# State-space stage with side products in halves over a chunk's four parts and a unit product of 384 columns; stage set-up of semaphores by five engines

## The chip, the cores and the metric

The kernel runs on one core of a Trainium2 chip. A core has TensorE (PE), VectorE (DVE), ScalarE (ACT), GpSimd (POOL) and SyncE (SP), each with a queue of its own that runs in order; they wait for each other through semaphores. The metric is the device time of one execution in microseconds (us); lower is better. 0.2% of it is 13 us.

## What is computed

The reference is two transformer-like layers over x of 128 rows of 64 tokens with 128 features. The change bears on the first block, a state-space block:

```python
normed = rmsnorm(x, input_norm_w)
xp = normed @ in_proj_W
x_z, z = (xp[..., :E], xp[..., E:])                       # E = 256
xc = silu(conv(x_z, conv_W) + conv_b)                     # four taps along time
dt = clip(softplus(xc @ dt_W + dt_b), 0.001, 0.1)
Bp, Cp = xc @ B_W, xc @ C_W                               # 64 states
A = -exp(A_log)
def step(h, x_t, dt_t, B_t, C_t):                         # 64 steps in time, one after the other
    h = exp(dt_t[..., None] * A) * h + dt_t[..., None] * B_t[:, None, :] * x_t[..., None]
    return h, einsum('ben,bn->be', h, C_t)
x = x + (y * silu(z)) @ out_proj_W
```

After it come a gated MLP, attention over a context, attention and a mixture of eight experts, grouped-query attention, attention with a mask, and a mixture of encoder layers.

## The kernel before

The program is a row of 14 stages. Each stage allocates its semaphores (`Stage.semaphore`, line 78), passes a barrier of all engines (`begin`, line 66), runs, clears the semaphores and passes a second barrier. A freshly allocated semaphore is raised to 1 by an instruction of GpSimd, one for each, between the two barriers.

The state-space stage (`mamba`, line 900) takes 16 chunks of 512 tokens (8 rows of 64 tokens). A chunk has 64 steps in time, which the code cuts in four parts j of 16 steps tl. For one step the state of 8 rows, 256 channels and 64 states lies as 128 partitions x 1024 columns in two PSUM banks; two pairs of banks take turns. A unit is the work of one step:

- PE: `products` multiplies the step sizes out to 1024 columns (line 1149, into the banks DT) and the input dt x B (line 1164, into the state's banks); `add_decayed` (by_quarters, line 1132) adds the decayed state of the columns `PE_PART`, with an identity as weights; `contract` (line 1181) multiplies the state products by C into the bank YB.
- ACT: `decay` (line 1381), the exponential of the step sizes into dA, three units ahead.
- DVE: `decay_pe_part` (line 1739) multiplies dA and the state for `PE_PART`; `decay_part` (line 1746) does so for the two `DVE_PARTS`; `add_part` (line 1755) adds the decayed state for these two in PSUM.

`PE_PART` is 256 columns and `DVE_PARTS` are 512 and 256 (lines 1020 and 1021). DVE's order in a unit t is: product of `PE_PART` (t), the two additions (t-1), the two products (t). It waits before the first of these for PE's `add_decayed` of unit t-1. PE's input product of unit t+1 waits for DVE's last product of unit t.

Between the units PE does side products for what comes next, all in the one bank PJ, so that ACT must copy each result out before the next is written: `turn` (transposes x), `conv` (four taps, one of 512 columns at a time), `gates` (z, 256 columns), `project_dt`, `project_c`, `turn_u` and `project_bc` (the parts' inputs), `turn_y` and `project_out` (the output). Their places are written out by hand in `chunk` for each engine: in part 0 dt (tl 7 to 10) and C (12, 13) of the next chunk; in part 2 the turn (8) and the first half of the channels' conv (10 to 13) of the chunk after that; in part 3 the second half (7 to 10) and the gates (11 to 15). ACT's copies stand at steps of their own, after `decay` of the same step. Where a product is copied out one unit and the bank used in the next, PE waits: this is called a hand-over below.

GpSimd multiplies the gates (`gated`), and makes the step size (`step_size`, line 1600) from the dt product in 11 instructions over 1024 columns, of which three add a constant to `lp` (line 1621). It splits the inputs in three bf16 pieces. SP loads x and the residual and spreads the pieces over partitions by 21 DMAs a part (`spread_pieces`).

`loop` runs chunk 0, then a hardware loop of three rounds with four chunks each, then the last three chunks.

Of the kernel before, what the change touches and what calls it, by code (L numbers as in the profile page):

```python
# [58 lines left out]
class Stage:  # L59


    def __init__(self, nc, sems, mem, name):
        self.nc, self.mem, self.name, self.handles = nc, mem, name, []
        mem.callback(self.end)
# [835 lines left out]
def mamba(nc, sems, ps, dram, x_in, x_out):  # L900
# [5 lines left out]
    LP_STEPS = 11  # L906
# [3 lines left out]
    with ExitStack() as mem:  # L910
# [67 lines left out]
        in_done = st.counter("in_done", 4)  # L978
        in_taken = st.counter("in_taken", 4)
        tanh_ready = st.counter("tanh_ready", 4)  # L980
        xz_scaled = st.counter("xz_scaled", 4)
        xz_ready = st.counter("xz_ready", 4)
# [5 lines left out]
        lp_step = st.counter("lp_step", LP_STEPS)  # L988
# [31 lines left out]
        PE_PART = slice(768, 1024)  # L1020
        DVE_PARTS = [slice(0, 512), slice(512, 768)]
# [16 lines left out]
        def loop(eng, chunk, first, last):  # L1038
            first()
            chunk(0, 0, True, True, False)  # L1040
            with looped(nc, eng, 0, (CHUNKS - 4) // 4) as r:
                for v in range(4):
                    chunk(4 * r + (1 + v), (1 + v) % 2, True, True, True)
            for i in range(CHUNKS - 3, CHUNKS):
                chunk(i, i % 2, i + 1 < CHUNKS, i + 2 < CHUNKS, True)
# [3 lines left out]
        with nc.Block() as block:  # L1049

            @block.sync
            def _(sp):
# [49 lines left out]
                def chunk(i, u, lead, lead2, trail):  # L1102
                    load_res(i, 0)
                    if trail:
                        spread_pieces(i, 1)
                        store(i - 1, 3)
                    load_res(i, 1)
# [6 lines left out]
                    if lead2 and not (isinstance(i, int) and i == CHUNKS - 3):  # L1114
                        load_x(i + 3)
# [12 lines left out]
            def _(pe):  # L1128
# [63 lines left out]
                def conv(i, f, k):  # L1192
                    if k == 0:
                        if f == 0:
                            pe.wait_ge(xT_ready.sem, xT_ready.at(i))
                        else:
                            pe.wait_ge(in_taken.sem, in_taken.at(i, 1))
                    mm = by_quarters(ps[:, PJ, :], w_conv[:, k, 128 * f:128 * f + 128], xT[:, :, k:k + 64], k == 0, k == 3)
                    if k == 3:
                        mm.then_inc(in_done.sem, 1)  # L1200

                def gates(i, j):
                    if j % 2 == 0:
                        pe.wait_ge(in_taken.sem, in_taken.at(i, 2 + j // 2))
# [3 lines left out]
                    if n == 1:  # L1208
                        mm.then_inc(in_done.sem, 1)

                def project_dt(i, u, e, f):
                    if e == 0:
                        pe.wait_ge(xz_ready.sem, xz_ready.at(i, f + 1))
                    if f == 0:
                        if e == 1:
                            pe.wait_ge(dtp_taken.sem, dtp_taken.at(i, 1))
                    mm = by_quarters(ps[:, PJ, :], w_dt[:, f, 128 * e:128 * e + 128], xz[:, u, 512 * f:512 * f + 512],
                                     f == 0, f == 1)
                    if f == 1:
                        mm.then_inc(dtp_done.sem, 1)  # L1220

                def project_c(i, u, f):
                    if f == 0:
                        pe.wait_ge(dtp_taken.sem, dtp_taken.at(i))
                    mm = by_quarters(ps[:, PJ, :], w_c2[:, f], xz[:, u, 512 * f:512 * f + 512], f == 0, f == 1)
                    if f == 1:
# [28 lines left out]
                def first():  # L1255
# [4 lines left out]
                    for i in range(2):  # L1260
# [3 lines left out]
                        for f in range(2):  # L1264
                            for k in range(4):
# [2760 lines left out]
```

## Time and profile before

| what | us |
|---|---|
| median of 3 runs | 6489.89 (6489.69 to 6494.92) |
| the profiled execution | 6484.01 |
| span of its trace | 6482.2 |
| end of the state-space stage | 2404 |

The profile is of one execution. Its page gives the busy share of each engine, the span in 40 slices and the costliest groups of instructions. The trace behind it answers as a timeline (start, length, instruction, and in brackets the idle time before it with what ended it), as groups by line, and as a table of windows. A PE row of "x8" holds 4 weight loads and 4 matmuls or 8 matmuls that were merged; the lengths of matmuls are modelled and overlap, so the distance from one start to the next is what counts. DVE rows overlap by some 0.06 us, for the same reason.

### The profile page before, as it was taken

The page shows a single profiled execution, that of the slowest core. Times are in us where ns is not written, and L with a number is a line of the kernel's source. Part 1 is how long each engine was busy: PE and PEld are TensorE (multiplying, and loading weights), DVE is VectorE, ACT ScalarE, POOL GpSimd, SP SyncE. Part 2 cuts the span into 40 slices and gives each one's busy share as a digit, 9 for nine tenths or more (in the row PEclk, how much of TensorE's full clock was granted, in tenths as well). Part 3 has the DMA queues.
Part 4 walks back from the last instruction along what each step waited for, and adds up shares of the span by engine and source line. Part 5 has one row for each costly group of instructions (what it writes and reads, how often), then busy time and mean ns, then how long its engine had stood idle before and what let it go on. Part 6 is the DMA issues. An engine that isn't in the chain of part 4 may idle for free. (4 is left out here: it accounts for less than half of the span.)

```text
span 6482.2 us, 173452 instructions
## 1 busy us (share of the span) xinstructions
PE 5026.5 (78%) x60580; PEld 2983.8 (46%) x60580; DVE 4987.2 (77%) x10255; ACT 3330.0 (51%) x4888; POOL 3321.4 (51%) x3031
## 2 busy tenths in 40 slices
PE   4889888988889875886868966999856648777890
PEld 1333333333333333564655534666645436666440
DVE  2999999999999984897965355777679928888334
ACT  3666666666666643555741202444446517777440
POOL 6544444545444413665634573555523329888443
PEclk8999999999999997998979977999978859999995
DMA  1111111111111112221123631000011012222443
GB/s 39 46 48 46 50 42 50 42 50 43 50 47 44 48 47 78 56 57 34 42 67 101 142 107 34 17 17 17 12 36 31 26 52 73 72 75 71 128 131 104
DMA packets 620485, 368.02 MB, mean 57 GB/s; under 512 B 67337, under 2 KB 601292, under 8 KB 619852
## 3 DMA queue, kind: packets, MB, share of 16 engines
q1 hardware_dynamic: 600524, 335.54, 18.6%
q0 software_dynamic: 11648, 21.26, 1.7%
q8 instruction: 352, 5.77, 0.4%
q10 hardware_dynamic: 7680, 3.15, 0.2%
q14 instruction: 281, 2.30, 0.1%
HBM read 204.83 MB, written 66.85 MB: 42 GB/s over the span
## 5 line engine op out<-in xcount | busy, mean ns | idle before, releaser
L1381 ACT ACTIVATE mb_dA<-ps,mb_a_neg 128x1024 f32<-128x1024 f32 x1008 | 1123.1, 1114 | 852.1 <-PE ps L1149 693.7
L1746 DVE TENSOR_TENSOR mb_m<-mb_dA,ps 128x512 f32<-128x512 f32 x2016 | 1015.6, 543 | 0.0
L1755 DVE TENSOR_TENSOR ps<-mb_m,ps 128x512 f32<-128x512 f32 x1984 | 1008.8, 552 | 0.0
L1132 PE MATMUL ps<-mb_m,mb_ident 128*32 128x256 f32 x7936 | 637.3, 393 | 2.9 <-DVE mb_m L1739 1.7
L1181 PE MATMUL ps<-mb_m,mb_cz 128*32 128x256 f32 x8064 | 624.3, 381 | 17.2 <-DVE mb_m L1746 6.5
L1164 PE MATMUL ps<-mb_ur,mb_bl 64*128 64x256 bf16 x4032 | 391.6, 273 | 160.3 <-DVE mb_m L1746 155.3
L1739 DVE TENSOR_TENSOR mb_m<-mb_dA,ps 128x256 f32<-128x256 f32 x1008 | 413.9, 411 | 72.0 <-PE ps L1132 45.0
L1149 PE MATMUL ps<-mb_ur,mb_sel 64*128 64x256 bf16 x4032 | 397.7, 276 | 28.6 <-DMA mb_ur<-mb_pc 15.6
L1181 PEld LDWEIGHTS ps<-mb_m,mb_cz 128*32 128x32 f32 x8064 | 256.1, 110 | 206.9 <-issue 34.7
L677 POOL TENSOR_TENSOR x_p<-x_p,x_rec 128x2048 f32<-128x2048 f32 x64 | 231.7, 3620 | 211.4 <-DVE x_rec L838 211.4
L1149 PEld LDWEIGHTS ps<-mb_ur,mb_sel 64*128 64x128 bf16 x4032 | 115.1, 94 | 485.0 <-ACT mb_dA L1381 288.1
L1164 PEld LDWEIGHTS ps<-mb_ur,mb_bl 64*128 64x128 bf16 x4032 | 156.8, 94 | 311.1 <-DVE mb_m L1746 298.3
L1660 POOL TENSOR_TENSOR mb_ys<-mb_ys,mb_cbu 128x256 f32<-128x256 f32 x64 | 46.8, 732 | 472.9 <-ACT mb_ys L1471 472.9
L677 POOL TENSOR_TENSOR ea_p<-ea_p,ea_rec 128x2048 f32<-128x2048 f32 x70 | 253.5, 3621 | 39.7 <-DVE ea_rec L838 39.1
L3187 POOL TENSOR_TENSOR gq_qr<-gq_qc,gq_qs 128x1024 f32<-128x1024 f32 x64 | 150.9, 2358 | 237.1 <-DVE gq_qs L3234 219.8
L1132 PEld LDWEIGHTS ps<-mb_m,mb_ident 128*32 128x32 f32 x7936 | 156.5, 108 | 217.9 <-DVE mb_m L1739 124.6
L2518 POOL DMA_INDIRECT mx_tk<-moe_normed,moe_tokens x156 | 147.5, 945 | 163.1 <-POOLq L68 103.3
L487 PE MATMUL ps<-x_ident,x_p 128*128 128x128 f32 x1024 | 164.1, 312 | 64.3 <-POOL x_p L677 64.3
L599 ACT ACTIVATE x_p<-x_p 128x2048 f32<-128x2048 f32 x64 | 122.0, 1906 | 166.3 <-DVE x_p L828 166.3
L606 ACT COPY x_pT<-ps 128x1024 f32<-128x1024 f32 x128 | 129.2, 1009 | 138.1 <-PE ps L487 137.1
L1647 POOL TENSOR_TENSOR mb_rest<-mb_tm,mb_pc 128x768 f32<-128x768 f32 x64 | 105.6, 1650 | 184.4 <-ACT mb_pc L1449 184.4
L606 ACT COPY ea_pT<-ps 128x1024 f32<-128x1024 f32 x140 | 141.6, 1012 | 99.4 <-PE ps L487 97.5
(493 smaller groups left out, 13198.9 us busy)
## 6 DMA issues: line engine op xcount, KB each, us to landing
mb_ur<-mb_pc SPq DMA_DIRECT2D x768, 64.0 KB
mb_bl<-mb_pc SPq DMA_DIRECT2D x576, 64.0 KB
ef_w<-in_ef_w SPq DMA_DIRECT2D x35, 514.5 KB
mx_w<-in_mx_w SPq DMA_DIRECT2D x39, 384.0 KB
moe_made<-mx_y SPq DMA_DIRECT2D x39, 256.0 KB, 2.4
ea_wqk<-in_ea_wqk SPq DMA_DIRECT2D x70, 129.0 KB
ea_wvo<-in_ea_wvo SPq DMA_DIRECT2D x70, 128.5 KB, 2.1
ea_x<-hidden SPq DMA_DIRECT2D x280, 32.0 KB, 2.0
```

The lines of the kernel that those rows point to most:

```text
L487: mm = nc.tensor.transpose(ps[:, 6 + c0 // 512, c0 % 512:c0 % 512 + 128], P_g[:, u, g, t, 2 * jj:2 * jj + 2, :].rearrange("p h k -> p (h k ...
L606: nc.scalar.copy(pT[:, t], ps[:, 6:8, :].rearrange("p a n -> p (a n)")).then_inc(pT_ready.sem, 1)
L677: nc.gpsimd.tensor_tensor(v, v, rec[:].rearrange("p (c a) -> p c a", a=1).to_broadcast([128, 32, 64]), ALU.mult).then_inc(p_ready.sem, 1)
L1132: mm = nc.tensor.matmul(out[c:c + 32], weights[:, c:c + 32], moving, start=start, stop=stop, skip_group_check=not grouped)
L1149: mm = nc.tensor.matmul(ps[:, DT + g, 256 * pl:256 * pl + 256], sel[k, pl], ur[k, t // 16 % 2, t % 16], start=True, stop=True)
L1164: mm = nc.tensor.matmul(ps[:, UB + 2 * ((t + v) % 2) + g, 256 * pl:256 * pl + 256], bl[k, s, tl, 128 * pl:128 * pl + 128], ur[k, s, tl], s ...
L1181: mm = nc.tensor.matmul(ps[32 * pr:32 * pr + 32, YB, 0:E], cz[:, j % 2, pr, 32 * tl:32 * tl + 32], m[:, t % RING, 256 * pr:256 * pr + 256] ...
L1381: nc.scalar.activation(dA[:, t % RING].rearrange("p (g n) -> p g n", g=2), ps[:, DT:DT + 2, :], ACT.Exp, scale=a_neg[:, 0:1]).then_inc(dA_ ...
L1739: nc.vector.tensor_tensor(m[:, t % RING, PE_PART], dA[:, t % RING, PE_PART], state(u, t - 1, PE_PART), ALU.mult).then_inc(mp_ready.sem, 1)
L1746: nc.vector.tensor_tensor(m[:, t % RING, cols], dA[:, t % RING, cols], state(u, t - 1, cols), ALU.mult).then_inc(md_ready.sem, 1)
L1755: nc.vector.tensor_tensor(h, m[:, t % RING, cols], h, ALU.add).then_inc(hd_ready.sem, 1)
L3187: nc.gpsimd.tensor_tensor(qr[:, t], qc[:, t], qs[:, t], ALU.add).then_inc(q_turned.sem, 1)
```

## The change

1. `PE_PART` becomes 384 columns, `DVE_PARTS` 320 and 320.
2. conv, dt and C products are made in halves of 256 columns, one a step, at steps 8 to 15. The parts change: part 0 has the turn, the gates and the first three quarters of C; part 1 the last of C and the conv of the first channels; part 2 the conv of the others; part 3 dt. x and z have semaphores of their own. dt, conv and gates are made two chunks ahead, C one; the dt products of chunk 1 are made before chunk 0 starts.
3. ACT's copies and tanh, and GpSimd's gates and norm, move with them. GpSimd makes the step size in two halves of 512 columns, 22 instructions, and adds the constants as `p * 1.0 + c`.
4. SP loads x of chunk i+3 earlier in chunk i.
5. A new semaphore is raised by GpSimd, SP, ACT, DVE and PE in turn.
6. Three later stages (experts, join, grouped-query attention) load their weights from ACT's queue in place of SP's.

```diff
     def semaphore(self, name):
         sem = self.nc.alloc_semaphore(name=f"{self.name}_{name}")
+        self.engines[len(self.handles) % 5].sem_inc(sem, 1)
         self.handles.append(sem)
-        self.nc.gpsimd.sem_inc(sem, 1)
...
-        PE_PART = slice(768, 1024)
-        DVE_PARTS = [slice(0, 512), slice(512, 768)]
+        PE_PART = slice(640, 1024)
+        DVE_PARTS = [slice(0, 320), slice(320, 640)]
...
-                def conv(i, f, k):
...
-                    mm = by_quarters(ps[:, PJ, :], w_conv[:, k, 128 * f:128 * f + 128], xT[:, :, k:k + 64], k == 0, k == 3)
+                def conv_tap(i, f, n):
+                    half, k = n // 4, n % 4
...
+                    mm = by_quarters(ps[:, PJ, cols], w_conv[:, k, 128 * f:128 * f + 128], xT[:, rows, k:k + 64],
+                                     k == 0, k == 3)
...
+                def side(i, u, j, tl, lead, trail):
...
+                        if j == 0 and lead:
+                            pe.wait_ge(dtp_taken.sem, dtp_taken.at(i + 1))
+                        elif j == 1 and lead:
+                            pe.wait_ge(cn_ready.sem, cn_ready.at(i + 1))
+                        elif j >= 2 and lead >= 2:
+                            pe.wait_ge(conv_taken.sem, conv_taken.at(i + 2, j - 1))
...
+                    if j == 0:
+                        if lead >= 2:
+                            if tl == 8:
+                                turn(i + 2)
...
+                            if tl in (10, 11, 12, 13):
+                                gates(i + 2, tl - 10)
+                        if lead and tl == 14:
+                            if lead >= 2:
+                                pe.wait_ge(gates_taken.sem, gates_taken.at(i + 2))
+                            project_c(i + 1, 1 - u, 0)
+                            project_c(i + 1, 1 - u, 1)
+                        if lead and tl == 15:
+                            project_c(i + 1, 1 - u, 2)
+                    elif j == 1:
+                        if lead and tl == 0:
+                            project_c(i + 1, 1 - u, 3)
+                        if lead >= 2 and tl >= 8:
+                            conv_tap(i + 2, 0, tl - 8)
+                    elif lead >= 2 and tl >= 8:
+                        if j == 2:
+                            conv_tap(i + 2, 1, tl - 8)
+                        else:
+                            project_dt(i + 2, u, (tl - 8) // 4, (tl - 8) % 4)
...
+                                ins = nc.gpsimd.tensor_scalar(p, p, 1.0, LOG1P[4 - n // 2], ALU.mult, ALU.add)
```

A unit with a side product on PE, in a chunk before (part 3, step 7, where the second channels' conv begins):

```order
L1132 MATMUL ps<-mb_m,mb_ident 32x256 [waits mb_mp_ready]
L1132 MATMUL ps<-mb_m,mb_ident 32x256 x3
L1181 MATMUL ps<-mb_m,mb_cz 32x256 [waits mb_md_ready,mb_mp_ready]
L1181 MATMUL ps<-mb_m,mb_cz 32x256 x3
L1132 MATMUL ps<-mb_xT,mb_w_conv 32x512 [waits mb_in_taken,mb_y_ready]
L1132 MATMUL ps<-mb_xT,mb_w_conv 32x512 x3
L1149 MATMUL ps<-mb_ur,mb_sel 128x256 [waits mb_dA_ready]
L1149 MATMUL ps<-mb_ur,mb_sel 128x256 x3
L1164 MATMUL ps<-mb_ur,mb_bl 128x256 [waits mb_md_ready]
L1164 MATMUL ps<-mb_ur,mb_bl 128x256 x3
```

The same engine now, in part 3, step 12, where the second column of dt begins:

```order
L1139 MATMUL ps<-mb_m,mb_ident 32x384 [waits mb_mp_ready]
L1139 MATMUL ps<-mb_m,mb_ident 32x384 x3
L1188 MATMUL ps<-mb_m,mb_cz 32x256 [waits mb_md_ready,mb_mp_ready]
L1188 MATMUL ps<-mb_m,mb_cz 32x256 x3
L1139 MATMUL ps<-mb_xz,mb_w_dt 32x256 [waits mb_dtp_taken]
L1139 MATMUL ps<-mb_xz,mb_w_dt 32x256 x3
L1156 MATMUL ps<-mb_ur,mb_sel 128x256 [waits mb_dA_ready]
L1156 MATMUL ps<-mb_ur,mb_sel 128x256 x3
L1171 MATMUL ps<-mb_ur,mb_bl 128x256 [waits mb_md_ready]
L1171 MATMUL ps<-mb_ur,mb_bl 128x256 x3
```

The added decay has 384 columns, the side product 256, and it waits for ACT's copy of the unit before; ahead of it nothing of PE's can run. On DVE, two units before:

```order
L1739 TENSOR_TENSOR mb_m<-mb_dA,ps 128x256 [waits mb_hp_ready,mb_y_summed,mb_dA_ready]
L1755 TENSOR_TENSOR ps<-mb_m,ps 128x512 [waits mb_md_ready,mb_ub_done]
L1755 TENSOR_TENSOR ps<-mb_m,ps 128x256 [waits mb_md_ready]
L1746 TENSOR_TENSOR mb_m<-mb_dA,ps 128x512 [waits mb_hd_ready]
L1746 TENSOR_TENSOR mb_m<-mb_dA,ps 128x256 [waits mb_hd_ready]
```

and now:

```order
L1784 TENSOR_TENSOR mb_m<-mb_dA,ps 128x384 [waits mb_hp_ready,mb_y_summed,mb_dA_ready]
L1800 TENSOR_TENSOR ps<-mb_m,ps 128x320 [waits mb_md_ready,mb_ub_done]
L1800 TENSOR_TENSOR ps<-mb_m,ps 128x320 [waits mb_md_ready]
L1791 TENSOR_TENSOR mb_m<-mb_dA,ps 128x320 [waits mb_hd_ready] x2
```

The order is the same and so are the waits; only the widths moved. On ACT, at the end of part 0 now, the copies of the gates and of C stand one behind the other in the units (L1397 is the exponential of a unit):

```order
L1397 ACTIVATE mb_dA<-ps,mb_a_neg 128x1024 [waits mb_md_ready,mb_dt_done] x2
L1427 ACTIVATE mb_raw<-ps 128x512 [waits mb_z_ready,mb_gates_done]
L1397 ACTIVATE mb_dA<-ps,mb_a_neg 128x1024 [waits mb_md_ready,mb_dt_done] x2
L1427 ACTIVATE mb_raw<-ps 128x512 [waits mb_z_ready,mb_gates_done]
L1397 ACTIVATE mb_dA<-ps,mb_a_neg 128x1024 [waits mb_md_ready,mb_dt_done] x3
L1445 COPY mb_cn<-ps 128x512 [waits mb_cz_ready,mb_c_proj]
L1494 COPY mb_ys<-ps 128x256 [waits mb_yzT_done,mb_y_summed]
```

Before, dt and C stood in this part and the gates in part 3; each copy still comes behind the exponential of its unit.

## Rows read from the trace of the kernel before

**Rows 1.** The page, section 1: busy us, share of the span and instructions by engine.

```profile
PE 5026.5 (78%) x60580; PEld 2983.8 (46%) x60580; DVE 4987.2 (77%) x10255; ACT 3330.0 (51%) x4888; POOL 3321.4 (51%) x3031
```

**Rows 2.** Table of windows: window and length in us, busy (instructions) by engine, PEclk, DMA.

```profile
484.00:626.00 142.00, 127.35 (x1816) 53.79 (x1813) 139.33 (x323) 90.96 (x117) 67.84 (x53) 1.00 0.18 47
```

**Rows 3.** Line L1583, once a chunk: ns min/median/max, and start of first and last.

```profile
L1583 POOL TENSOR_TENSOR mb_nrstd<-mb_nrstd,mb_half_neg x1: 1041/1041/1041, 1616.8 to 1616.8; 128x4 f32<-128x4 f32 x1
...
L1583 POOL TENSOR_TENSOR mb_nrstd<-mb_nrstd,mb_half_neg x1: 1041/1041/1041, 1758.3 to 1758.3; 128x4 f32<-128x4 f32 x1
```

**Rows 4.** Timeline of DVE, one unit: start us, length us, instructions, idle before.

```profile
938.00 0.41 DVE L1739 TENSOR_TENSOR mb_m<-mb_dA,ps 128x256 f32<-128x256 f32 x1
...
940.19 0.41 DVE L1739 TENSOR_TENSOR mb_m<-mb_dA,ps 128x256 f32<-128x256 f32 x1
```

**Rows 5.** Timeline of PE: a unit with a whole side product, hand-overs, a half one.

```profile
949.15 0.65 PE L1132 MATMUL ps<-mb_w_bc,mb_xz 128*32 128x128 f32 x16 [0.54 <-ACT mb_tm L1435]
949.72 0.39 PE L1149 MATMUL ps<-mb_ur,mb_sel 64*128 64x256 bf16 x4
...
965.10 0.39 PE L1149 MATMUL ps<-mb_ur,mb_sel 64*128 64x256 bf16 x4
965.33 0.38 PE L1164 MATMUL ps<-mb_ur,mb_bl 64*128 64x256 bf16 x4
965.64 0.64 PE L1132 MATMUL ps<-mb_m,mb_ident 128*32 128x256 f32 x8
966.10 0.61 PE L1181 MATMUL ps<-mb_m,mb_cz 128*32 128x256 f32 x8
966.53 1.04 PE L1132 MATMUL ps<-mb_xT,mb_w_conv 128*32 128x512 f32 x8
967.51 0.39 PE L1149 MATMUL ps<-mb_ur,mb_sel 64*128 64x256 bf16 x4
...
969.76 0.64 PE L1132 MATMUL ps<-mb_w_in,mb_xT_tok 128*32 128x256 f32 x8 [0.65 <-ACT mb_raw L1403]
...
971.76 0.62 PE L1132 MATMUL ps<-mb_w_in,mb_xT_tok 128*32 128x256 f32 x8
972.31 0.39 PE L1149 MATMUL ps<-mb_ur,mb_sel 64*128 64x256 bf16 x4
```

**Rows 6.** Timeline of DVE: its waits at the change of chunk and later.

```profile
980.22 0.42 DVE L1739 TENSOR_TENSOR mb_m<-mb_dA,ps 128x256 f32<-128x256 f32 x1 [0.72 <-PE ps L1132]
...
1002.00 0.42 DVE L1739 TENSOR_TENSOR mb_m<-mb_dA,ps 128x256 f32<-128x256 f32 x1 [0.46 <-PE ps L1132]
```

**Rows 7.** Groups of DVE, 300 to 2200 us: count, busy us, mean ns, idle before.

```profile
L1755 DVE TENSOR_TENSOR ps<-mb_m,ps 128x512 f32<-128x512 f32 x829 | 568.3, 686 | 0.0
L1755 DVE TENSOR_TENSOR ps<-mb_m,ps 128x256 f32<-128x256 f32 x829 | 347.5, 419 | 0.0
```

**Rows 8.** Where the loop enters anew: a window, then DVE's timeline.

```profile
836.00:840.00 4.00, 3.15 (x24) 1.36 (x20) 2.28 (x5) 1.95 (x4) 1.45 (x2) 0.50 0.34 89
...
837.35 0.42 DVE L1739 TENSOR_TENSOR mb_m<-mb_dA,ps 128x256 f32<-128x256 f32 x1 [2.83 <-PE ps L1132]
```

**Rows 9.** Timeline of GpSimd and PE in the stage's start.

```profile
65.07 1.05 POOL L1617 TENSOR_SCALAR mb_lp<-mb_ex 128x1024 f32<-128x1024 f32 x1 [0.20 <-POOL mb_ex L1615]
...
68.76 2.78 POOL L1621 TENSOR_SCALAR mb_lp<-mb_lp 128x1024 f32<-128x1024 f32 x1 [0.20 <-POOL mb_lp L1609]
...
91.18 1.09 PE L1233 MATMUL ps<-mb_ident,mb_du 128*128 128x128 f32 x4 [15.26 <-POOL mb_du L1611]
```

**Rows 10.** Line L81, the increments: the first stage, then all stages.

```profile
L81 POOLq EVENT_SEMAPHORE  x56: 17/17/17, 0.9 to 5.2; - x56
...
L81 POOLq EVENT_SEMAPHORE  x524: 17/17/17, 0.9 to 6317.0; - x175
```

**Rows 11.** Timeline of the grouped-query stage's start.

```profile
3910.79 0.35 SPq L2913 DMA_DIRECT2D gq_ident<-in_ident  x1
...
3914.51 0.43 SPq L2917 DMA_DIRECT2D gq_x<-hidden  x1
```

More of the change, by code:

```diff
@@ L1100, in first, with chunk @@
                     spread_pieces(0, 1)
-                def chunk(i, u, lead, lead2, trail):
+                def chunk(i, u, lead, trail):
                     load_res(i, 0)
@@ L1286, in chunk @@
+                def chunk(i, u, lead, trail):
                     for t in range(T):
-                        j, tl = t // 16, t % 16
-                        k = 4 * i + j
                         if 1 <= t < T - 1:
@@ L1348, in chunk @@
[L1348 to L1360 removed]
+                        side(i, u, t // 16, t % 16, lead, trail)
@@ L1494, in first @@
                             take_conv(i, f)
+                            tanh_of_x(i, i, f)
+                        if i == 0:
+                            for e in range(2):
+                                take_dt(0, e)
                         for half in range(2):
@@ L1510, in first, with chunk @@
                     decay(0, 2)
-                def chunk(i, u, lead, lead2, trail):
+                    for e in range(2):
+                        take_dt(1, e)
+                    for j in range(4):
+                        norm(2, j)
+                def chunk(i, u, lead, trail):
                     for t in range(T):
@@ L1684, in first, with chunk @@
                         split_lo(0, j)
-                def chunk(i, u, lead, lead2, trail):
+                    for f in range(2):
+                        gate_x(1, 1, f)
+                    norm_scale(2)
+                    step_size(1, 1, 0, 4)
+                def chunk(i, u, lead, trail):
                     for t in range(T):
                         j, tl = t // 16, t % 16
+                        if j == 0 and tl == 2 and lead >= 2:
+                            scale(i + 2)
                         if tl == 1 and (j > 0 or trail):
@@ L1772, in first, with chunk @@
                     weigh_bc(0, 1)
-                def chunk(i, u, lead, lead2, trail):
-                    for t in range(T):
+                def chunk(i, u, lead, trail):
+                    for t in range(1, T):
                         j, tl = t // 16, t % 16
-                        if t >= 1:
-                            decay_pe_part(i, u, t)
+                        decay_pe_part(i, u, t)
                         if t >= 2:
@@ L2565, in _ @@
             def _(act):
+                for dst, src in loads:
+                    act.dma_start(dst, src).then_inc(w_loaded.sem, 16)
                 def take(i):
@@ L2727, in _ @@
             def _(act):
+                for dst, src in loads:
+                    act.dma_start(dst, src).then_inc(w_loaded.sem, 16)
                 for i in range(CHUNKS):
@@ L2911, in _ @@
             def _(sp):
-                for dst, src in loads:
-                    sp.dma_start(dst, src).then_inc(w_loaded.sem, 16)
                 def lead(i, u):
@@ L3102, in _ @@
             def _(act):
+                for dst, src in loads:
+                    act.dma_start(dst, src).then_inc(w_loaded.sem, 16)
                 def take_x(i, u):
```

396 lines of the change are left out of this document (194 added, 202 removed).

## Prediction

> **What bounds the kernel now.** I read the page first [rows 1]: in the span of 6482.2 us PE is 78% and DVE 77% busy, no engine at its limit over the whole. So the question is the state-space stage, the first 2400 us, and there the table of windows [rows 2]: in 142 us DVE works 139.33 us, PE shows 127.35 and the granted clock is 1.00. DVE is the bound of this stage. One chunk (512 tokens, 63 units) takes 141.5 us: the once-a-chunk power of the norm stands at 1616.8 and at 1758.3 [rows 3]. The DVE timeline [rows 4] shows a unit without waits, from one first product to the next: 938.00 to 940.19, 2.19 us. PE's own unit, from rows where it never waits for DVE [rows 5], is step size 0.23 (965.10 to 965.33), input 0.31, added decay 0.46, contraction 0.43: 1.43 us. A side product of 512 columns adds 0.98 (966.53 to 967.51), so a unit with one takes 2.41, more than DVE's 2.19; one of 256 columns adds 0.55 (971.76 to 972.31). PE has slack in the sum (1.43 x 63 plus the side work, against 141.5) but not in such stretches, and DVE's few waits are for PE [rows 6]: 0.72 at the change of chunk, 0.46 in the stretch of dt products.
>
> **Unit product of 384 columns.** Of DVE's five instructions a unit the three products together stay at 1024 columns; the two additions fall from 768 to 640. 512 against 256 columns is 686 against 419 ns [rows 7]: 267 ns for 256 columns, so 128 columns are 133 ns. With 62 additions a chunk DVE falls by 8.2 us, from 139.3 to 131.1. On PE the added decay grows by 128 columns. A side product shows the price of 256 columns, 0.98 less 0.55 = 0.43 [rows 5], so 128 are 0.21 us: the unit goes to 1.64.
>
> The Trainium skill (VectorE: DVE Perf Modes, The TRN2 errata) speaks against this edit: it tells us to keep tiles at 512 columns or more, since each instruction pays a fixed part. Here the count of instructions stays at five, and rows of this trace give the fixed part either way, so the sum is 8.2 by the row and 8.3 by the page's slope of one column in 1/0.96 ns; I take the row.
>
> **Side products in halves.** Per chunk PE then has: 63 x (0.23+0.31+0.43) = 61.1; 62 x 0.67 = 41.5; 32 half products (16 conv, 8 dt, 4 gates, 4 C) x 0.55 = 17.6; 17 short steps (turns, B/C, output) at the price of the B/C projection, 0.57 (949.15 to 949.72) [rows 5], 9.7. Sum 129.9, one per cent under DVE's 131.1: the two engines tie. What is not hidden then are PE's waits for ACT. A bank handed over (PE product, ACT copy, PE again) shows 0.65 idle at 969.76, and the B/C projection 0.54 at 949.15 [rows 5]. The new order has a hand-over from one unit to the next in four places a chunk (between the two dt columns, between the halves of the gates, gates to C, C to the turn) and four B/C projections. PE reaches them 0.2 later than now, which leaves about 0.6 and 0.5 each: 4 x 0.6 + 4 x 0.5 = 4.4. On the other side PE can't run ahead of DVE, since the input product waits for DVE's last product of the unit: in units 3, 5 and 7 of each part, which have no side work (1.64 against 2.06), it gains 0.42 each, 1.26 a part, and can use of this only the lag of some 0.55 that the stretch before has left: 0.7 is lost, 2.9 a chunk. PE's chunk: 129.9 + 4.4 + 2.9 = 137.2; I take 137.5. In DVE's terms these are 6.4 us of waits a chunk where there are 2.2 now. Gain 4.0 a chunk, in 14 chunks 56 us. Bounds: 133.5 (DVE's 131.1 and its present 2.2, the hand-overs hidden) and 141.5 (nothing gained).
> The last two chunks carry next to no side products; there I take DVE's 8.2 less 2: 12 us.
> Three times the loop enters anew; a wait of 2.83 and 4 us at a granted clock of 0.50 are seen there [rows 8], the slow one of the two levels, after PE had stood still. With PE in the lead each of the units at that clock costs more: +4 in all.
> GpSimd gets no slower: its 11 steps become 22 of half width, but the three additions of a constant, 2.77 us, take the form of the multiply-add, 1.05 [rows 9]. SyncE's four x loads come earlier in its queue, ahead of the second spread of pieces, which waits for unit 12 of PE anyway: nothing. ACT's count of copies is unchanged.
>
> **Start of the stage.** PE's first turn of u stands 15.26 us for GpSimd's step sizes and starts at 91.18 [rows 9]. The additions' new form saves 3 x 1.7 = 5.2 on that chain, the z gates (5.1) leave it, half-width overheads cost about 2; then eight dt products of the second chunk are put ahead of unit 1, some 5 us at the low clock. Net -4, between -12 and +4.
>
> **Set-up by five engines.** GpSimd issues 524 increments in 14 stage set-ups [rows 10]; the 56 of the first stand from 0.9 to 5.2, 78 ns each, and all other engines stand at the barrier. 524 x 0.08 = 42 us. With a fifth each, in parallel at the same pace, 8.5 us stay: -33. No row shows the pace of another engine's increment. From above the whole 42 can't be beaten by more than its four fifths; from below I take PE at 200 ns, twice and a half GpSimd's, and its 105 then leave 21: -20. I take -33, GpSimd's row being the same instruction.
> The Trainium skill (Advanced Engine Details and Errata, DMA Bandwidth Details) puts an increment's overhead at about one cycle on this chip. By that the set-ups cost nothing now and the change gains nothing there; the forecast would be 33 higher, 6418. The row of 78 ns decides against it, and the page speaks of DMA.
>
> **Weights on ACT's queue.** In the grouped-query stage eight weight loads stand ahead of the first x load: 3910.79 to 3914.51 [rows 11], and PE's first work needs that x load. On two queues that is about -3.5; in the experts' stage two loads are 0.9, mostly hidden; in the join PE starts on the weights themselves: 0. Sum -4, between 0 and -6.
>
> **Sum.** -56 -12 +4 -4 -33 -4 = -105 us. The profiled execution took 6484.01, 1.8 more than its span; it goes to 6379. The median is 5.9 above it: 6489.9 - 105 = 6385.
>
> **Rivals.**
> Hand-overs hidden: PE is late less often than I count, the chunk falls to 133.5, DVE stays the bound. For it: only a wait that ends after DVE's own unit counts, and PE may lag by about 0.6 us before DVE waits. Against it: eight half products in a row use up that lag. 14 x 4 more: 6329.
> PE as the bound without gain: the chunk stays at 141.5 because each PE unit costs 0.07 more than its rows (a switch between two kinds of product). Only set-up, tail and start are won: 6441.
> The other side, slower: the added decay is a link in a chain, DVE product to PE to the next DVE product, and has 0.21 us more in each unit. Its margin is DVE's unit less the input product, the added decay's full length and some 0.2 of signals: 2.19 - 0.31 - 0.64 - 0.2 = 1.0 us now, 2.06 - 0.31 - 0.85 - 0.3 = 0.6 after (0.3, since PE must also wait for a longer DVE product). With each ACT copy that comes late all beyond it goes to DVE. That decides once a chunk takes over 146 us, since the other terms bring 49: all four hand-overs, the B/C projections and 0.1 more in each of the 63 units. At 148 it gives 6489.9 - 49 + 91 = 6532. Against it: no stretch now loses more than 0.8 at a time.
> That set-up isn't won (the increments overlap with the barrier anyhow): 6418.
>
> **Chances.** Forecast 0.50; hand-overs hidden 0.22; no gain in the chunk 0.16; set-up not won 0.06; slower 0.06. The range runs from 6320 to 6448: it takes in 6329 and 6441, and the lower bound of the set-up on the forecast; about 0.06 is left out below and 0.12 above. About 0.2%, 13 us, is what a measurement of this kernel can tell from no change: faster by more 0.92, within it 0.04, slower 0.04.
>
> **What will show it.** Right: the once-a-chunk power every 137 to 138 us; DVE 131 busy of it, its waits at the 384-column product, most of them in units 12 to 18 of the first part and at the change of chunk; PE's idle before the dt, gates, C and turn steps near 0.6; the increments of the first stage done by about 1.8 us; later stages unchanged in length. Wrong: DVE waits under 3 us a chunk (first rival), or the PE unit without side work above 1.70 and with a half above 2.25 (second and third), or barriers that still stand over 2 us.

## The result, and the profile after

The changed kernel takes 6448.17 us (median of 4 runs, 6440.6 to 6455.99) against 6490.6 of the kernel before, measured beside it: a ratio of 0.9933, with a 95% interval from 0.9916 to 0.9951. It is 42 us faster, where the prediction had 105. The range ended at 6448, so the median lies 0.2 above its end, which is within the noise; the gain of 42 in place of 105 is not. The number of the rival "PE as the bound without gain" (6441) is near the measured one, but its mechanism is only a part of what happened: the experiments below show that PE's own work does not fill the chunk.

The chunk first. The once-a-chunk power of the norm (its line is L1606 now; columns as in [rows 3]) stands at:

```profile
L1606 POOL TENSOR_TENSOR mb_nrstd<-mb_nrstd,mb_half_neg x1: 1041/1041/1041, 677.6 to 677.6; 128x4 f32<-128x4 f32 x1
...
L1606 POOL TENSOR_TENSOR mb_nrstd<-mb_nrstd,mb_half_neg x1: 1041/1041/1041, 818.5 to 818.5; 128x4 f32<-128x4 f32 x1
```

That is 140.9 us a chunk, where [rows 3] has 141.5 and the forecast 137.5. The page's first section, as [rows 1]:

```profile
PE 5171.6 (80%) x62372; PEld 3072.5 (48%) x62372; DVE 4875.8 (76%) x10255; ACT 3332.8 (52%) x4888; POOL 3274.3 (51%) x3207
```

and the table of windows over one chunk, as [rows 2]:

```profile
681.00:822.00 141.00, 135.24 (x1918) 59.12 (x1920) 131.94 (x321) 90.59 (x116) 64.89 (x64) 1.00 0.19 47
```

The 139.33 of [rows 2] belong to a window of 142 us. A window of one chunk of the kernel before, 141.5 us, is:

```profile
1187.50:1329.00 141.50, 126.84 (x1804) 53.51 (x1804) 138.83 (x323) 90.46 (x116) 67.83 (x54) 1.00 0.17 47
```

So DVE's work fell from 138.8 to 131.9, by 6.9 us (the forecast had 8.2, from 139.3 to 131.1). But it now stands idle for 9 us of every chunk, where it did for 2.7. The table of waits over the same chunk says for whom (engine, line and product, who released it: us in all, times, longest):

```profile
DVE mb_m L1784 <- PE ps L1139: 8.5, 11, 1.6
PE ps L1188 <- issue: 2.3, 3, 1.1
PE ps L1139 <- ACT mb_tm L1458: 1.3, 4, 0.3
PE ps L1139 <- ACT mb_raw L1427: 0.7, 2, 0.3
PE ps L1156 <- ACT mb_dA L1397: 0.5, 1, 0.5
PE ps L1139 <- ACT mb_ex L1450: 0.4, 1, 0.4
```

DVE waits 8.5 us for PE, and PE in turn waits for ACT's copies. DVE's waits lie at the change of chunk (1.60 and 0.44), at the gates and at C in part 0 (0.20 and 1.02), in the first two units of part 1 (1.49 and 0.58), in those of parts 2 and 3 (0.70 and 0.58 in each), and behind dt (0.56). Two of them:

```profile
683.94 0.56 DVE L1784 TENSOR_TENSOR mb_m<-mb_dA,ps 128x384 f32<-128x384 f32 x1 [1.60 <-PE ps L1139]
...
715.12 0.56 DVE L1784 TENSOR_TENSOR mb_m<-mb_dA,ps 128x384 f32<-128x384 f32 x1 [1.02 <-PE ps L1139]
```
 The largest of PE's waits, at L1188 (the contraction), is put down to "issue", so no name leads to it. PE's timeline at the start of part 1 shows it (columns as in [rows 5]):

```profile
698.29 0.61 PE L1188 MATMUL ps<-mb_m,mb_cz 128*32 128x256 f32 x8
698.83 0.65 PE L1196 MATMUL ps<-mb_ident,mb_xn 128*128 128x128 f32 x4
...
702.40 0.61 PE L1188 MATMUL ps<-mb_m,mb_cz 128*32 128x256 f32 x8
702.83 0.61 PE L1139 MATMUL ps<-mb_w_in,mb_xT_tok 128*32 128x256 f32 x8
...
718.58 0.85 PE L1139 MATMUL ps<-mb_m,mb_ident 128*32 128x384 f32 x8
720.51 0.64 PE L1188 MATMUL ps<-mb_m,mb_cz 128*32 128x256 f32 x8 [1.08 <-issue]
...
728.83 0.85 PE L1139 MATMUL ps<-mb_m,mb_ident 128*32 128x384 f32 x8
729.50 0.61 PE L1188 MATMUL ps<-mb_m,mb_cz 128*32 128x256 f32 x8
730.04 0.39 PE L1156 MATMUL ps<-mb_ur,mb_sel 64*128 64x256 bf16 x4
730.27 0.38 PE L1171 MATMUL ps<-mb_ur,mb_bl 64*128 64x256 bf16 x4
730.58 0.85 PE L1139 MATMUL ps<-mb_m,mb_ident 128*32 128x384 f32 x8
```

and ACT's, just ahead of it:

```profile
718.55 1.11 ACT L1397 ACTIVATE mb_dA<-ps,mb_a_neg 128x1024 f32<-128x1024 f32 x1 [1.08 <-PE ps L1156]
719.57 0.58 ACT L1445 COPY mb_cn<-ps 128x512 f32<-128x512 f32 x1
720.03 0.38 ACT L1494 COPY mb_ys<-ps 128x256 f32<-128x256 f32 x1
```

The first contraction of a part writes the bank YB anew, so it must wait until ACT has copied the last part's sums out (`take_y`, L1494). That copy stands behind an exponential of 1.11, and in part 1 behind the copy of C too. The last rows show a unit of PE without side work: 728.83 to 730.58, 1.75 to 1.77, where the forecast had 1.64. The contraction takes 0.54 there (729.50 to 730.04), and 0.43 ahead of a side product with weights of 128 x 32 like its own (702.40 to 702.83). It takes 0.54 ahead of a transpose too, whose operands are fp32 as its own are but whose weights are 128 x 128 (698.29 to 698.83).

Between the two profiled executions the 43.2 us split so (DVE's first product of a chunk is the mark in the first three rows; the first chunk is in the first row):

| stretch | before | after | difference | forecast |
|---|---|---|---|---|
| start, to the first product of chunk 1 | 264.5 | 259.7 | -4.8 | -4, and -3 of set-up |
| the next 13 chunks | 1850.7 | 1839.0 | -11.7 | -56 (14 chunks) + 4 |
| the last two | 277.9 | 266.6 | -11.3 | -12 |
| from there to the stage's end | 11.3 | 11.1 | -0.2 | 0 |
| the 13 later stages | 4077.9 | 4062.6 | -15.3 | -30 of set-up, -4 of weights |

The first row hides two larger differences. DVE's first product of chunk 0 stands at 118.3 before and at 107.9 after, 10.4 earlier, 2.5 of it from the set-up. Chunk 0 itself, with eight dt products more on PE, takes 151.7 in place of 146.2.

The last row is not a sharp one: the grouped-query stage alone took between 798.6 and 817.8 us in the profiles of changed kernels that don't touch it, so the terms in it are read from medians below.

### The profile page after: what moved, and what is told of

The parts are those of the page before. It is cut to its first block and busy times, and to the rows that moved or that the text cites. A ratio compares the mean times of both kernels' runs of the same rounds, so it can differ in the third digit from the quotient of the medians.

```text
span 6439.0 us, 177583 instructions
## 1 busy us (share of the span) xinstructions
PE 5171.6 (80%) x62372; PEld 3072.5 (48%) x62372; DVE 4875.8 (76%) x10255; ACT 3332.8 (52%) x4888; POOL 3274.3 (51%) x3207
## 5 line engine op out<-in xcount | busy, mean ns | idle before, releaser
L1397 ACT ACTIVATE mb_dA<-ps,mb_a_neg 128x1024 f32<-128x1024 f32 x1008 | 1122.8, 1114 | 826.2 <-PE ps L1156 743.7
L1791 DVE TENSOR_TENSOR mb_m<-mb_dA,ps 128x320 f32<-128x320 f32 x2016 | 886.8, 482 | 0.0
L1800 DVE TENSOR_TENSOR ps<-mb_m,ps 128x320 f32<-128x320 f32 x1984 | 881.3, 491 | 0.0
L1139 PE MATMUL ps<-mb_m,mb_ident 128*32 128x384 f32 x7936 | 847.1, 499 | 12.2 <-DVE mb_m L1784 2.8
L1784 DVE TENSOR_TENSOR mb_m<-mb_dA,ps 128x384 f32<-128x384 f32 x1008 | 555.4, 551 | 166.3 <-PE ps L1139 115.5
L1188 PE MATMUL ps<-mb_m,mb_cz 128*32 128x256 f32 x8064 | 622.1, 380 | 42.4 <-issue 28.4
L1188 PEld LDWEIGHTS ps<-mb_m,mb_cz 128*32 128x32 f32 x8064 | 255.2, 110 | 439.5 <-issue 420.4
L1171 PEld LDWEIGHTS ps<-mb_ur,mb_bl 64*128 64x128 bf16 x4032 | 184.1, 94 | 67.3 <-DVE mb_m L1791 40.5
L3241 POOL TENSOR_TENSOR gq_p<-gq_p,gq_rec 128x2048 f32<-128x2048 f32 x32 | 115.8, 3620 | 128.9 <-DVE gq_rec L3318 128.9
```

The costliest lines, as they stand in the source:

```text
L1139: mm = nc.tensor.matmul(out[c:c + 32], weights[:, c:c + 32], moving, start=start, stop=stop, skip_group_check=not grouped)
L1171: mm = nc.tensor.matmul(ps[:, UB + 2 * ((t + v) % 2) + g, 256 * pl:256 * pl + 256], bl[k, s, tl, 128 * pl:128 * pl + 128], ur[k, s, tl], s ...
L1188: mm = nc.tensor.matmul(ps[32 * pr:32 * pr + 32, YB, 0:E], cz[:, j % 2, pr, 32 * tl:32 * tl + 32], m[:, t % RING, 256 * pr:256 * pr + 256] ...
L1397: nc.scalar.activation(dA[:, t % RING].rearrange("p (g n) -> p g n", g=2), ps[:, DT:DT + 2, :], ACT.Exp, scale=a_neg[:, 0:1]).then_inc(dA_ ...
L1784: nc.vector.tensor_tensor(m[:, t % RING, PE_PART], dA[:, t % RING, PE_PART], state(u, t - 1, PE_PART), ALU.mult).then_inc(mp_ready.sem, 1)
L1791: nc.vector.tensor_tensor(m[:, t % RING, cols], dA[:, t % RING, cols], state(u, t - 1, cols), ALU.mult).then_inc(md_ready.sem, 1)
```

## The experiments

Theory A: at these widths PE's own work and DVE's tie at about 132 us a chunk, and PE's waits for ACT come on top one for one. Theory B in its several forms: PE's work alone fills the chunk; the order costs time by itself; or the waits only change their name. The expectations of the first four runs (a1 to a4) take the whole difference of 141.0 and 131.9, 9.1 us, for waits for ACT; read from PE's timeline they are 7.1, as the section on why the prediction was wrong works out. All ratios are against the kernel before, run beside each; "chunk" is the steady distance of the norm's power in the profile.

| run | ratio (95%) | chunk us |
|---|---|---|
| the change | 0.9933 (0.9916 to 0.9951) | 141.0 |
| the same again (d2) | 0.9927 (0.9913 to 0.9940) | 141.0 |
| a1: output bank copied first | 0.9867 (0.9850 to 0.9883) | 138.6 |
| c1: five kinds of copies first | 0.9789 (0.9772 to 0.9805) | 134.3 |
| c2: c1 with 320 columns | 0.9821 (0.9804 to 0.9837) | 135.2 |
| a4: the change with 320 columns | 0.9901 (0.9884 to 0.9917) | 139.4 |
| a3: the change with 256 columns | 0.9948 (0.9931 to 0.9964) | 140.9 |
| c3: eight half products left out | 0.9892 (0.9875 to 0.9908) | 139.3 |
| b1: before with 384 columns | 1.0016 (1.0007 to 1.0026) | 142.9 |
| d4: before with copies first | 0.9954 (0.9940 to 0.9967) | 139.5 |
| a2: the change, GpSimd raises all | 0.9966 (0.9953 to 0.9978) | 141.0 |
| d1: before, five engines raise | 0.9957 (0.9943 to 0.9970) | 141.5 |
| d3: the change, weights on SP | 0.9928 (0.9914 to 0.9942) | 141.0 |

**Copy of the output bank ahead of the exponential (a1).** In ACT's `chunk`:

```diff
+                        if tl == 0 and behind:
+                            if j == 0:
+                                take_y(i - 1, 3)
+                            else:
+                                take_y(i, j - 1)
                         if t + 3 < T:
                             decay(i, t + 3)
...
-                        if tl == 0 and behind:
-                            if j == 0:
-                                take_y(i - 1, 3)
-                            else:
-                                take_y(i, j - 1)
```

> The changed kernel, with ACT's copy of the output bank (take_y) put ahead of the exponential of the same step instead of behind it. Theory A (PE and DVE tie at 131.9 us a chunk and what is lost are PE's waits for ACT, 9.1 us a chunk, 2.3 of them before the first contraction of parts 1 to 3): the chunk falls from 141.0 by about 2.3 to 138.7, the whole to about 32 us below the changed kernel. Theory B (PE's own work fills the chunk, a wait removed comes back as the next wait): the chunk stays within 0.5 of 141.0 and the whole within 7 us.

Measured: chunk 138.6, end of the stage 2343.9 instead of 2376.4 (-32.5), 6407.83 us. That is 40 below the change by the medians, 43 by the ratios (some 16 to either side), so the expected 32 fits; the stage's end in the two profiles is the sharper figure. In ACT's timeline the copy now runs before the exponential, beside PE's side product:

```profile
1129.89 0.37 ACT L1494 COPY mb_ys<-ps 128x256 f32<-128x256 f32 x1 [0.26 <-PE ps L1188]
1130.70 1.11 ACT L1397 ACTIVATE mb_dA<-ps,mb_a_neg 128x1024 f32<-128x1024 f32 x1 [0.44 <-PE ps L1156]
```

and the contraction follows PE's added decay without a wait:

```profile
1130.73 0.85 PE L1139 MATMUL ps<-mb_m,mb_ident 128*32 128x384 f32 x8
1131.40 0.61 PE L1188 MATMUL ps<-mb_m,mb_cz 128*32 128x256 f32 x8
```

For the chunk this is Theory A: 2.3 us of waits taken away are 2.3 us of the chunk.

**The other copies too (c1).** `take_c`, `take_u`, `take_gates` and the first `take_dt` are moved the same way:

```diff
+                        if j == 1 and tl == 0 and lead:
+                            take_c(i + 1, 1 - u)
+                        if tl == 1 and (j < 2 or lead):
+                            take_u(*((i, j + 2) if j < 2 else (i + 1, j - 2)))
+                        if j == 0 and lead >= 2 and tl in (11, 13):
+                            take_gates(i + 2, (tl - 11) // 2)
+                        if j == 3 and lead >= 2 and tl == 11:
+                            take_dt(i + 2, 0)
                         if t + 3 < T:
                             decay(i, t + 3)
...
```

> Take_y ahead of the exponential as in the run before, and with it ACT's other copies that PE waits for in its next unit: take_c, take_u, the gates', the first dt's. Theory A (PE's waits for ACT lie on the path one for one): of the 6.8 us a chunk that are left, 4.2 go (4 x 0.51 before B/C, 0.52 and 0.57 at the gates and C, 0.6 at dt, 0.5 at the turn of part 1); chunk 134.4 to 135.5 instead of 138.6, the whole 44 to 59 us below that run. Theory B (the exponential, put behind a copy of 0.6, is late for the next dt product or for DVE, so that a wait only changes its name): chunk 138 or more.

Measured: chunk 134.3, 6353.8 us (6350.24 to 6356.1), the fastest of all: 94 us below the change's 6448 (93 by the ratios). That is Theory A, just below its 134.4 to 135.5. The waits of PE's matmuls and of DVE in a stretch of 141 us of this kernel:

```profile
DVE mb_m L1786 <- PE ps L1139: 2.2, 3, 1.6
PE ps L1156 <- ACT mb_dA L1397: 0.5, 1, 0.5
DVE mb_m L1786 <- ACT mb_dA L1397: 0.2, 1, 0.2
```

A window of one chunk has DVE at 131.47 of 134.3 us. What is left of DVE's idle time is mainly the 1.6 at the change of chunk. In that unit DVE has no additions to do, which is the likely reason that it reaches its next product so early; no run tests it.

```profile
1066.00:1200.30 134.30, 133.17 (x1920) 60.00 (x1916) 131.47 (x321) 90.56 (x117) 64.90 (x64) 1.00 0.18 49
```

**The width, with and without the waits (c2, a4, a3).** The only edit is the width; for c2 and a4:

```diff
-        PE_PART = slice(640, 1024)
-        DVE_PARTS = [slice(0, 320), slice(320, 640)]
+        PE_PART = slice(704, 1024)
+        DVE_PARTS = [slice(0, 352), slice(352, 704)]
```

> The run before with a unit product of 320 columns. Theory A: with PE's waits gone the narrower product has nothing left to give: PE 125.4 + 2.6 = 128, DVE 135.5 and about 1 of waits, chunk 136.5, the whole 15 to 25 us above the run before. If waits of PE still rule at 384, it is level with or below the run before.

Measured: chunk 135.2, 6375.63 us, 22 above c1. With most of the waits gone 384 columns are the better width, and DVE is the bound at 320 (134.2 us of work in 135.2).

> The changed kernel with a unit product of 320 columns and two of 352 on DVE. Theory A: DVE 135.5, PE 131.9 less 6.5 = 125.4 and 9.1 of waits for ACT = 134.5, so both are near each other and the chunk is 137 to 138, 40 to 56 us below the changed kernel. Theory B (PE's work fills the chunk at any width near the tie, the waits add to DVE's work): 135.5 and DVE's 9 of waits = 144, slower than the changed kernel.

Measured: chunk 139.4, 6432.57 us. Neither theory's number: A had 137 to 138. DVE waits seven times in this chunk, 4.6 us together, although the expected sum of PE's work and waits (134.5) lies under DVE's expected 135.5. PE also waits for DVE in it, six times, 0.2 to 0.4 each. The sum of a whole chunk hides that, and the places of the waits suggest why: a wait at the start of a part reaches DVE before PE's spare time elsewhere in the chunk could make up for it, since PE's input product waits for DVE's last product of the unit before and can't be made ahead of it.

> The changed kernel with the unit product of 256 columns as before, so the half side products and the new order alone. Theory A: DVE is the bound again with 139.1 us a chunk, PE has 131.9 less 62 x 0.21 = 118.9 and its waits for ACT are hidden; chunk 140.0 (139.1 and under 1 us of waits), 14 us below the changed kernel in the stage's chunks. Theory B (the new order itself costs time whatever the widths): chunk 141.5 or more, the whole 7 us or more above the changed kernel.

Measured: chunk 140.9, 6460.57 us, so A's 140.0 was again a little low: four DVE waits, 2.2 us, of which 0.89 and 0.45 stand at the start of part 1. The new order by itself wins 0.6 of a chunk; the 384 columns as the change has them win nothing more in the steady chunk, and their gain is mainly the last two chunks. This run shows one thing more. With the old widths PE still waits 1.29 for the output bank at the start of part 1, behind the copies of C and of the bank:

```profile
1148.76 0.64 PE L1188 MATMUL ps<-mb_m,mb_cz 128*32 128x256 f32 x8 [1.29 <-issue]
```

So that wait came with the new order, which put the copy of C there, and not with PE's shorter distance to DVE.

**Less side work (c3).** Two of the conv's four taps return at once:

```diff
+                    if k in (1, 2):
+                        return
```

> The changed kernel with the second and third of the conv's four taps left out (8 of 16 half products a chunk; its output is another). Each takes 0.42 off PE, in parts 1 and 2. Theory A (PE's work and waits fill these parts, 35.1 us against 33.3 of DVE): each part falls to 33.4, the chunk to 137.6, the whole by 45 us to about 6403. Theory B (DVE waits for latencies at the start of a part, PE's load is no bound): the chunk stays at 141.0, the whole within 7 us of 6448.

Measured: chunk 139.3, 6419.21 us: half of what A expected. In the change part 1 runs from 723.13 to 758.23 by DVE's first products, 35.1; here it takes 34.3 (1139.19 to 1173.49). The kernel leaves two taps out, so its output differs; it serves for its time alone. The units with and without conv all go at DVE's pace now, but at the start of a part two units still take 2.44 and 2.73. So 0.8 of the 1.7 us that PE saved is won and in the rest PE waits for DVE: its weight loads stand 10.0 us for DVE's 384-column product in a stretch of 141 us, where they stood 5.4 in the change. Work and waits of PE do not form one pool: room in the middle of a part does not pay for a wait at its start.

**The width alone on the kernel before (b1).**

```diff
-        PE_PART = slice(768, 1024)
-        DVE_PARTS = [slice(0, 512), slice(512, 768)]
+        PE_PART = slice(640, 1024)
+        DVE_PARTS = [slice(0, 320), slice(320, 640)]
```

> The kernel before with the unit product of 384 columns and nothing else of the change. PE there has 121.4 us a chunk without waits, 134.4 with the wider product; whole side products of 0.98 in a row make units of 2.6 against DVE's 2.06, and the waits for ACT (0.5 to 1.2 each, about 5 a chunk) come on top. Theory A: chunk 140 to 142, so that the wider product alone wins nothing, -20 to +10 us against before. Theory B (the width is the gain, the halves are not needed): DVE's 131.5 and its 2.2 of waits, chunk 134, 105 us below before.

Measured: chunk 142.9, ratio 1.0016, 10 us slower than before by it. Units with a whole side product take 2.62 on PE (columns as in [rows 5]) against DVE's 2.06:

```profile
1250.14 0.85 PE L1132 MATMUL ps<-mb_m,mb_ident 128*32 128x384 f32 x8
1250.81 0.61 PE L1181 MATMUL ps<-mb_m,mb_cz 128*32 128x256 f32 x8
1251.24 1.04 PE L1132 MATMUL ps<-mb_xT,mb_w_conv 128*32 128x512 f32 x8
1252.22 0.39 PE L1149 MATMUL ps<-mb_ur,mb_sel 64*128 64x256 bf16 x4
1252.44 0.38 PE L1164 MATMUL ps<-mb_ur,mb_bl 64*128 64x256 bf16 x4
1252.76 0.85 PE L1132 MATMUL ps<-mb_m,mb_ident 128*32 128x384 f32 x8
```

DVE waits 21 times in it, 0.5 on average:

```profile
DVE mb_m L1739 <- PE ps L1132: 10.9, 21, 1.4
```

With ACT's copies where they stand the wide product needs the halves and the new order; together they are worth 1.9 us a chunk more than the product alone. The wide product on the old order with the copies moved, as in c1, was not run.

**Copies first on the kernel before (d4).** The same kind of edit on the old order (`take_y`, `take_u`, the first `take_dt`, both of `take_gates`).

> The kernel before with five of ACT's copies ahead of the exponential (the output bank, take_u, the first dt's, both of the gates'). There PE has 20 us a chunk to spare against DVE. Theory A (PE's waits cost only where PE ties with DVE): DVE's waits at the change of chunk and in the dt stretch (0.72 and 0.46) shrink at most, chunk 140.3 to 141.5, 0 to 17 us below before. Theory B (these waits cost one for one in any kernel): 4 us a chunk, 60 us below before.

Measured: chunk 139.5, ratio 0.9954, 30 us. Below B's 60, yet beyond A's 17. Before, DVE waited five times in a chunk for PE, afterwards twice (the two tables of waits, before and d4):

```profile
DVE mb_m L1739 <- PE ps L1132: 2.7, 5, 0.7
```

```profile
DVE mb_m L1739 <- PE ps L1132: 1.1, 2, 0.7
```

I had counted two of these waits, [rows 6]; there were five. The rule behind it stands in both kernels: most of the change's 8.5 us of waits and of before's 2.7 come from ACT's place for its copies, and 6 of the former and 1.6 of the latter went when they were moved (the chunk fell by 6.7 and by 2.0). Slack over a whole chunk did not cover these waits in the kernel before, as Theory A had it.

**The set-up alone (a2, d1).** a2 raises all semaphores from GpSimd in the changed kernel; d1 gives the kernel before the five engines:

```diff
+        self.engines[len(self.handles) % 5].sem_inc(sem, 1)
...
-        self.nc.gpsimd.sem_inc(sem, 1)
```

> The changed kernel with the semaphores raised by GpSimd alone again. If the term of 33 us in the forecast holds, it is 33 us slower than the changed kernel. If PE's increments of about 150 ns, a fifth of them, set the end of each set-up (first stage 0.9 to 2.7 instead of 0.9 to 5.2), the gain was 15 to 25 us. If an increment costs next to nothing, 0 to 3 us.

> The kernel before with nothing but the set-up of semaphores by five engines. By the forecast 33 us faster. By the increments in the traces of before and after, the 14 set-ups take 40.8 us before and 15.5 after, PE's last increment being the end of each: 25 us faster (ratio 0.9961). If the increments lay beside something else that holds the barrier, under 10 us.

Measured: a2 0.9966, d1 0.9957. Against the change's 0.9933 the first says 21 us (with the noise of two ratios, some 14 to either side), the second 28 (19 to 37); the increments in the traces say 25. In the fifth stage, which has 70 semaphores, the increments before stood from 2975.5 to 2980.9; those of the changed kernel:

```profile
L81 POOLq EVENT_SEMAPHORE  x14: 17/17/17, 2944.2 to 2945.2; - x14
L81 SPq EVENT_SEMAPHORE  x14: 17/17/17, 2944.2 to 2945.0; - x14
L81 ACTq EVENT_SEMAPHORE  x14: 17/17/17, 2944.2 to 2945.1; - x14
L81 DVEq EVENT_SEMAPHORE  x14: 21/21/21, 2944.2 to 2945.4; - x14
L81 PEldq EVENT_SEMAPHORE  x14: 51/51/51, 2944.3 to 2946.3; - x14
```

PE takes 150 ns for each (2.0 us for 13 steps), the others 60 to 95, and PE's last one ends the set-up. The 14 set-ups sum to 40.8 us before and 15.5 after.

**The weights (d3), and the change again (d2).**

```diff
                 @block.sync
+                for dst, src in loads:
+                    sp.dma_start(dst, src).then_inc(w_loaded.sem, 16)
...
                 @block.scalar
-                for dst, src in loads:
-                    act.dma_start(dst, src).then_inc(w_loaded.sem, 16)
```

> The changed kernel with the weight loads of the three later stages on SP's queue again. By the forecast 4 us slower than the changed kernel (0 to 6); under 4 us it can't be told from no change, except by the length of the grouped-query stage's start in the trace. If the loads on ACT's queue cost ACT more than SP gains, it is faster.

> The changed kernel itself once more, on the same chip as the three others, so that they can be set against it: 42 us below before (ratio 0.9935).

Measured: d3 0.9928, d2 0.9927, no difference that these runs could show; their intervals are 9 us to either side, so 4 us would not be seen. The start of the grouped-query stage tells more than the total. In the changed kernel, its first load, its last weight and PE's first work:

```profile
3872.38 0.38 SPq L2958 DMA_DIRECT2D gq_x<-hidden  x1
...
3875.88 0.49 ACTq L3145 DMA_DIRECT2D gq_alibi<-in_g_alibi  x1
...
3883.04 0.69 PE L2995 MATMUL ps<-gq_ident,gq_x 128*128 128x128 f32 x2 [32.30 <-DMA gq_alibi<-in_g_alibi]
```

PE starts 10.7 us after the first load, released by the last weight. Before, the first load stands at 3910.79 [rows 11] and PE's first matmul at 3919.86: 9.1. In d2 and d3, on one chip, it is 10.95 with ACT's queue and 9.44 with SP's. So two queues made this stage's start 1.5 us longer: PE waits for all the weights anyway, and it starts 7.2 us after the issue of the last of them, which now goes beside the x loads, where it started 5.35 after the issue of the x load behind the weights before.

## Why the prediction was wrong, step by step

- **What bounds the kernel: right.** DVE before, near a tie after, and the chunk of the state-space stage, where the forecast looked, is also where most of the miss lay.
- **DVE's own work: near, from a wrong start.** 131.1 forecast, 131.9 measured. The forecast took the 139.3 of a window of 142 us for a chunk of 141.5; the chunk has 138.8, and the fall was 6.9 and not 8.2. By the same slip it gave the kernel before 2.2 of waits for its 2.7. From one first product to the next a unit did fall by the 0.13 that the rows gave (2.19 to 2.06). 384 columns take 551 ns and 320 take 482 or 490. The Trainium skill (VectorE: DVE Perf Modes, The TRN2 errata) warns of tiles under 512 columns; at an unchanged count of instructions the work of a chunk fell by 5% all the same.
- **PE's unit: the term that was mis-sized first.** The step "contraction 0.43" came from a unit with a side product behind the contraction. Ahead of the product of the step sizes it takes 0.54, in the 15 units a chunk that have no side work, and so it does ahead of the transposes. The former is 1.7; with the transposes and some tenths elsewhere PE's work is 132.4 (141.0 less the waits below) and not 129.9, so it is level with DVE and not 1% under it. The unit with a half product was right: 2.19. The reason that the rival "without gain" gave, a switch between two kinds of product, is thus borne out in part: 2.5 us in 63 units is 0.04 each, where it had 0.07.
- **PE's waits for ACT: the step that failed.** It read "four places a chunk and four B/C projections", 4.4 us. Measured by how much the distances between starts exceed their usual ones, the B/C waits were 2.0 (right), the hand-overs at gates, C and dt 1.7 (2.4 forecast for four), one for an exponential at the change of chunk 0.6. What was missing is the bank YB: the first contraction of parts 1 to 3 waits for `take_y`, 1.08 and twice 0.59 in the rows, 2.8 by distances. In all 7.1. The wait had been there before, at 0.16, as "issue":

```profile
1193.47 0.64 PE L1181 MATMUL ps<-mb_m,mb_cz 128*32 128x256 f32 x8 [0.16 <-issue]
```

  At part 1 the new place of the C copy made it long (1.29 at the old widths too, run a3); at parts 2 and 3 it was still 0.16 in a3 and became 0.59 with the 384 columns. a1 shows its price: 32 us at the stage's end. The fourth hand-over of the forecast, C to the turn, is not seen by itself, since the wait for YB stands just ahead of it.
- **PE can't run ahead: right as a mechanism.** It was priced at 2.9 a chunk; about 1.5 of waits for DVE remained in the change. a4 and c3 show it at work: 1.4 to 2 us a chunk more than the sums of work and waits gave.
- **The chunk's sum** was therefore 137.2 where 141.0 came: 2.5 more work, 2.7 more waits for ACT, 1.4 less for DVE. The share of each is a reading of distances in one trace; a1 and c1 test the waits, nothing tests the work. I had taken 137.5, and the 3.5 in 14 chunks are 49 of the 62 us by which the profiled executions differ from -105. "Nothing gained" had been given 0.16 and "hand-overs hidden" 0.22; c1 at 134.3 shows that the latter was nearly reachable (133.5), by moving five kinds of copies and not by itself.
- **The last two chunks: right** (-12, measured -11.3). **Start: near** (-4, measured -2.3 without the set-up: 7.9 earlier to the first product, and 5.5 lost in chunk 0 where the forecast had 5 for the dt products ahead of unit 1). No run takes these terms apart. **Loop re-entries: wrong sign, small.** Forecast +4; the four chunks around the two re-entries take 8.5 us more than steady ones, 11.6 before. Why is open.
- **Set-up: mechanism right, size off.** -33 forecast, 21 to 28 measured. I took GpSimd's 78 ns for all engines; PE's is 150 ns. The bound of 200 ns gave -20, so it lay within the bounds stated. The Trainium skill (Advanced Engine Details and Errata, DMA Bandwidth Details) has about one cycle for an increment; the rows above show 60 to 150 ns on every engine.
- **Weights: wrong for the stage that the term came from.** There the start became 1.5 longer, where I had -3.5; for the whole the runs can't tell -4 from 0. The step "PE's first work needs that x load" left out that it also needs every weight.
- **Not slower: right.** The added-decay chain did not bind by itself: every wait of DVE for PE in the chunk shown of the change follows a wait of PE for ACT, or that and the change of chunk, and b1's 21 stand in stretches of whole side products and behind PE's waits for ACT.
- **The signs.** The list of what would show it pointed two ways. DVE's 8.5 us of waits ruled out the first rival. The PE unit without side work, 1.77, passed the 1.70 that was to speak for the second and third, while the one with a half stayed at 2.19, below 2.25. The first stage's increments ended at 2.7 on PE in place of 1.8. Of DVE's waits 2.6 us stand at the starts of parts 2 and 3, where none was foreseen.

## What to carry to other kernels

When an edit brings two engines to a tie, the small waits of the engine that had slack become the kernel's time: those that a1 and c1 took away, 2.3 and then 4.2 us a chunk, gave 2.3 and 4.3. Slack in the sum of a chunk is no safeguard either, as d4 showed with 30 us in a kernel without a tie. List every bank and buffer that a third engine must free, also those whose wait is short now or is shown without a releaser, and price each at the new, shorter unit. Where a copy frees what the partner needs next and the longer work of the same step feeds something units ahead, put the copy first: that was worth 94 us here, more than twice the whole change. And read a unit's price from a unit that has the same neighbours as the one it is used for.

## What the runs showed of the hardware

- An fp32 matmul group of 256 columns with weights of 128 x 32 was followed after 0.43 us by a group with weights of the same shape, and after 0.54 us by one with weights of 64 x 128 (bf16) or of 128 x 128 (fp32). So the type of the next group is not what decides; whether it is the shape, no run varies by itself.
- Raising a semaphore took 150 ns on PE's queue, about 95 on DVE's, 80 on GpSimd's and 60 to 70 on SP's and ACT's, though the record of each is 17 to 51 ns long.
- A GpSimd `tensor_scalar` over 512 fp32 columns as `p * 1.0 + c` took 0.62 us. Over 1024 columns a multiplication and an addition in one instruction took 1.05 and the plain addition 2.78 [rows 9]. GpSimd's busy time in a chunk fell from 67.8 to 64.9 us, though it has twice the instructions there.
